# Attention, the normalisation behind it and the last MLP's first half put into one block of a fused two-layer kernel

## The chip, the core and the metric

The kernel runs on one core of a Trainium2 chip. A core has a matrix engine (TensorE, PE in the rows), a vector engine (VectorE, DVE), a scalar engine (ScalarE, ACT), a general engine (GpSimd, POOL) and a queue that here only starts transfers (SyncE, SP). They run side by side, each takes its own instructions strictly in order, and they wait for each other with semaphores. The metric is the time of one execution on the device, in microseconds (us).

## The reference, cut to what matters

Two layers, each of an attention-like part and an MLP, with a layernorm before and behind each part. The change touches the end of the second attention and the second MLP (x is 4 x 256 tokens of 512, in f32).

```python
x = x + _layernorm(_L1_attn_ref(_layernorm(x), Wq, Wkr, Wdk, Wupk, Wupv, Wo))   # 32 heads of 128, 8 groups
x = x + _layernorm(_L1_ffn_ref(_layernorm(x), w1, mean_w1, w2, mean_w2, w3, mean_w3))

def _binary_diff_weight(w, base):
    d = w - base
    return base + jnp.mean(jnp.abs(d)) * jnp.sign(d)
W1, W2, W3 = ...                                  # each from its pair, 512 x 1792 elements
h = jax.nn.silu(hidden @ W1.T) * (hidden @ W3.T)  # 1792 wide
return h @ W2.T
```

The three means are computed long before, and lie in a small tile (coeff).

## The kernel before, in words

The program is a row of phases. Each is a block with one instruction list for each engine, and a barrier of all engines closes it. Tokens lie as 8 tiles of 128 rows; four batches of 256 tokens are two tiles each. Every large matmul is done as three (high part by high part, low by high, high by low), from operands that ScalarE rounds (the high part) and GpSimd or VectorE subtracts (the low part).

**Attention** (`attention_phase`, L1222): 8 groups of heads times 4 batches are 32 units. `groups` writes group 0 and group 7 out and loops over the others. A unit b of TensorE's body is: the queries of the next unit (48 matmuls of 256 columns, L1297), the output product of the unit before (24 of 512 columns, L1322 to L1324), the transposes of the probabilities and their product with the values (`attend`, L1331 to L1344), and the scores of the next unit (L1308, L1310). Around it ScalarE copies half of the query product aside (`turn`, L1368), GpSimd multiplies it by the sines (L1423), VectorE multiplies by the cosines and adds both (`rotate`, L1456), takes the row maxima (L1461 to L1468), ScalarE does the exponentials (L1377, L1380), VectorE scales them (`probabilities`, L1474 to L1479) and adds the output product to `acc` (L1485). Once a group, GpSimd subtracts the low part of a weight (L1427, L1431). The last unit, (7, 3), has no queries of another unit to cover its softmax.

**"fc"** (`finish_phase` without a product): for each of the 8 token tiles, VectorE takes mean and variance of `acc` (L348 to L352), GpSimd the inverse root (L304), VectorE scales, adds to `x` (L373, L376), takes the moments of the new `x`, and normalises (L333); TensorE transposes (L223), ScalarE and VectorE split the result into `xh` and `xl` (L257, L338). The first two tiles of the MLP's weights are loaded at its start (L208).

**"md"** (`widen_phase`, kind "diff"): 14 tiles of 128 hidden channels. For each, GpSimd subtracts base from weight into `full` (L569), ScalarE takes the sign (L516), VectorE makes base + mean x sign in three parts (L598), ScalarE and GpSimd split two of them into `wh` and `wl` (L523, L564), the third is kept in `down`; TensorE does 48 matmuls of 512 columns (L503), ScalarE the silu (L552) and VectorE the product into `hidden` (L618). Weights, `full`, `wh` and `wl` are held twice, so that GpSimd subtracts two tiles ahead. **"fd"** then does the last product, its norm and the stores.

## Time and profile before

| | us |
|---|---|
| median of 3 runs | 1897.51 |
| lowest, highest | 1897.16, 1898.31 |
| the profiled execution's own time | 1897.62 |
| its span, first to last instruction | 1895.8 |
| TensorE busy in the span | 1677.3 (88%) |
| VectorE, ScalarE, GpSimd busy | 1153.1, 859.2, 814.2 |

The profile is of one execution. Its span is 1.8 us shorter than that execution's time. A timeline row gives the start, the duration, the engine, the source line, the operation, what it writes and reads, how many of them are merged in the row, and in brackets how long the engine was idle before it and who ended that. A row of windows gives, for a stretch, the busy time of each engine, the TensorE clock granted (1.00 is 2.4 GHz, 0.50 is 1.2 GHz) and the share of the DMA engines that was busy.

### The profile page before, as it was taken

What the parts mean: (1) busy time and instruction counts of PE and PEld (TensorE: products, weight loads), DVE (VectorE), ACT (ScalarE), POOL (GpSimd) and SP (SyncE); (2) the same over time, 40 slices, a digit from 0 to 9 for tenths busy, and PEclk for the clock granted to TensorE, in tenths of its full rate; (3) what the DMA queues carried; (4) which work ended last, traced back from release to release, by engine and by line L of the source; (5) the groups of instructions that cost most, each with busy time, mean ns of one, the idle gap of its engine ahead of it and who ended that gap; (6) DMA issues with size and microseconds to landing.
All of it is one profiled execution on the core that took longest, in us unless ns stands there. A gap on an engine that the chain in (4) does not pass through costs nothing. (4 is left out here: it accounts for less than half of the span.)

```text
span 1895.8 us, 24327 instructions
## 1 busy us (share of the span) xinstructions
PE 1677.3 (88%) x8118; PEld 1372.5 (72%) x8118; DVE 1153.1 (61%) x1614; ACT 859.2 (45%) x1743; POOL 814.2 (43%) x416
## 2 busy tenths in 40 slices
PE   5984889899997799898989999999999996399988
PEld 4852777787776688676877778778878784288867
DVE  4325999999996432452816666666675666546332
...
DMA packets 25185, 100.79 MB, mean 53 GB/s; under 512 B 3104, under 2 KB 3360, under 8 KB 22560
## 3 DMA queue, kind: packets, MB, share of 16 engines
...
## 5 line engine op out<-in xcount | busy, mean ns | idle before, releaser
L1423 POOL TENSOR_TENSOR stretch_turned<-stretch_turned,res_const 128x1024 f32<-128x1024 f32 x32 | 79.9, 2496 | 402.6 <-ACT stretch_turned L1369 402.6
L985 PE MATMUL psum<-scratch_s,res_const 128*128 128x256 f32 x1024 | 247.5, 380 | 4.0 <-DVE scratch_s L957 4.0
L985 PEld LDWEIGHTS psum<-scratch_s,res_const 128*128 128x128 f32 x1024 | 194.1, 190 | 32.2 <-DVE scratch_s L957 6.0
L858 POOL TENSOR_TENSOR scratch_s<-scratch_s,scan_cm 128x1024 f32<-128x1024 f32 x64 | 150.9, 2357 | 54.0 <-DVE scratch_s L947 54.0
L947 DVE TENSOR_TENSOR_SCAN scratch_s<-psum,scratch_s 128x512 f32<-128x512 f32 x128 | 155.3, 1213 | 4.4 <-ACT psum L899 4.2
L1297 PE MATMUL psum<-opnd_xh,query_wqh 128*128 128x256 f32 x512 | 151.3, 295 | 1.9 <-PEq L94 1.9
L846 POOL TENSOR_TENSOR scratch_s<-scan_bm,scratch_s 128x1024 f32<-128x1024 f32 x64 | 151.0, 2360 | 0.1
L899 ACT ACTIVATE psum<-ssm_dt,ssm_vec 128x255 f32 (+1 forms) x256 | 111.2, 466 | 80.3 <-DVE scratch_s L947 79.8
L1297 PE MATMUL psum<-opnd_xh,query_wql 128*128 128x256 f32 x512 | 145.6, 284 | 0.0
L1297 PE MATMUL psum<-opnd_xl,query_wqh 128*128 128x256 f32 x512 | 145.6, 284 | 0.0
L979 PE MATMUL psum<-scan_diag,scratch_s 128*128 128x256 f32 x512 | 133.2, 384 | 0.5 <-ACT scratch_s L891 0.5
L1377 ACT ACTIVATE stretch_pa<-psum,stretch_nm 128x128 f32<-128x128 f32 x128 | 45.3, 366 | 194.7 <-DVE stretch_nm L1468 194.7
L979 PEld LDWEIGHTS psum<-scan_diag,scratch_s 128*128 128x128 f32 x512 | 96.2, 193 | 13.0 <-ACT scratch_s L891 0.9
L1322 PE MATMUL psum<-stretch_woh,stretch_oh 128*128 128x512 f32 x256 | 100.3, 392 | 1.4 <-DVE stretch_ol L1501 1.4
L1297 PEld LDWEIGHTS psum<-opnd_xh,query_wqh 128*128 128x128 f32 x512 | 98.9, 193 | 3.2 <-issue 2.3
L1323 PE MATMUL psum<-stretch_wol,stretch_oh 128*128 128x512 f32 x256 | 100.0, 391 | 0.0
L1324 PE MATMUL psum<-stretch_woh,stretch_ol 128*128 128x512 f32 x256 | 99.9, 390 | 0.0
L1297 PEld LDWEIGHTS psum<-opnd_xl,query_wqh 128*128 128x128 f32 x512 | 98.8, 193 | 0.8
L1297 PEld LDWEIGHTS psum<-opnd_xh,query_wql 128*128 128x128 f32 x512 | 98.8, 193 | 0.0
L957 DVE TENSOR_TENSOR scratch_s<-psum,scan_cm 128x512 f32<-128x512 f32 x128 | 88.6, 692 | 14.2
L235 PE MATMUL psum<-stretch_wh,stretch_hh 128*128 128x512 f32 x176 | 71.0, 404 | 16.9 <-ACT stretch_wh L284 15.2
L503 PE MATMUL psum<-opnd_xh,mlp_wh 128*128 128x512 f32 x224 | 70.1, 394 | 14.9 <-POOL mlp_wl L564 14.9
...
## 6 DMA issues: line engine op xcount, KB each, us to landing
...
```

Of the source, the lines that this page charges most:

```text
L846: nc.gpsimd.tensor_tensor(by_state(shared[r][h]), bm[:, 4 * h:4 * h + 4, :], u[r].rearrange("p (a t) -> p a t", a=1).broadcast_to((P, 4, S ...
L858: nc.gpsimd.tensor_tensor(shared[r][h], shared[r][h], weights(4 * h, 4), ALU.mult).then_inc(weighted_pool, 1)
L899: ins = nc.scalar.activation(by_state(bank)[:, n, 1:SEQ], flat_dt[:, bass.ds(s * SEQ + 1, SEQ - 1)], ACT.Exp, scale=M.vec[:, bass.ds(s * N ...
L947: nc.vector.tensor_tensor_scan(quarter(r, i), decay_shared[i % 2], quarter(r, i), 0.0, ALU.mult, ALU.add).then_inc(scanned, 1)
L957: nc.vector.tensor_tensor(own[i], state[i], weights(NH + 2 * i, 2), ALU.mult).then_inc(weighted, 1)
L979: mm = nc.tensor.matmul(by_state(state[i])[:, :, t * P:(t + 1) * P], ut[r][:, t * P:(t + 1) * P], diag[:, t, 2 * i:2 * i + 2, :], start=Tr ...
L985: mm = nc.tensor.matmul(ps_y[r], ident, part[:, n * SEQ:(n + 1) * SEQ], start=False, stop=stop and (n + 1) * SEQ == part.shape[1])
L1297: mm = nc.tensor.matmul(ps_q[:, h * SEQ:(h + 1) * SEQ], w[:, k, h * HD:(h + 1) * HD], x[:, k, b * SEQ:(b + 1) * SEQ], start=(k == 0 and w ...
L1322: nc.tensor.matmul(X[t], oh[:, t, part], woh[:, h, :], start=(h == 0), stop=False)
L1323: nc.tensor.matmul(X[t], oh[:, t, part], wol[:, h, :], start=False, stop=False)
L1324: mm = nc.tensor.matmul(X[t], ol[:, t, part], woh[:, h, :], start=False, stop=(h == HPG - 1))
L1423: nc.gpsimd.tensor_tensor(heads(turned[:, :]), heads(turned[:, :]), over_heads(C_SIN, SEQ), ALU.mult).then_inc(q_sine, 1)
```

## The change

The phases of attention, "fc" and "md" become one block, `attention_mlp_phase`. The steps of "fc" and of the first MLP weights are written between the steps of attention's last group, and behind them. ScalarE applies both normalisations (`y_norm`, `x_norm`), GpSimd adds to `x` (`residual`). Weights are held in two slots, each with one raw and one base tile: the first slot lies over keys of groups 0 to 4, the second over the query weights. Difference, sign and sum are made in place in the raw tile. A slot is loaded again once its low part and its `down` part are made. MLP tiles 0 and 1 are run batch by batch (`widen_batch`, 24 matmuls of 256 columns for both products of a batch) as tokens become ready; tiles 2 to 13 as before, 48 matmuls each. GpSimd makes the difference of a tile behind the low part of the tile before. `ending(g, b, at)` is true in group 7 at unit b == at.

```diff
+    HALVES = ((0, 0, 2, 3), (1, 0, 4, 7), (0, 1, 5, 6), (1, 1, 2, 3))
+    ps_m = [[M.ps[:, 4 * s + 2 * a:4 * s + 2 * a + 2, :].rearrange("p a c -> p (a c)") for a in range(2)] for s in range(2)]
...
+            def load_mlp(f):
+                s = f % 2
+                if f == 0:
+                    sp.wait_ge(scored, U - BATCH)
+                if f == 1:
+                    sp.wait_ge(wo_lo, GROUPS)
+                    sp.wait_ge(q_prod, U)
+                at_least(sp, mw_lo, f - 1)
+                at_least(sp, mw_down, f - 1)
+                sp.dma_start(mw_raw[s][:, :], w_mlp[:, f * RC:(f + 1) * RC]).then_inc(mw_in[s], 16)
+                sp.dma_start(mw_base[s][:, :], b_mlp[:, f * RC:(f + 1) * RC]).then_inc(mw_in[s], 16)
+
...
+            for f in range(F1):
+                load_mlp(f)
...
+            def token_transposes(t):
+
+                pe.wait_ge(xn_ready, t + 1)
+                if t < 2:
+                    pe.wait_ge(q_turned, U)
+                    pe.wait_ge(q_cosine, U)
+                at_least(pe, x_lo, t - 1)
+                for c in range(KM):
+                    mm = nc.tensor.transpose(ps_t[t][:, c * P:(c + 1) * P], xn[t % 2][:, c * P:(c + 1) * P], ident)
+                mm.then_inc(transposed, 1)
...
+            def widen_into(out, f, a, lo, hi):
+                for k in range(KM):
+                    for w, x in ((mwh, M.xh), (mwh, M.xl), (mwl, M.xh)):
+                        mm = nc.tensor.matmul(out, w[f % 2][:, a, k, :], x[:, k, lo:hi],
+                                              start=(k == 0 and w is mwh and x is M.xh), stop=(k == KM - 1 and w is mwl))
+                return mm
...
+            def widen_batch(i, b):
+
+                f, _, *banks = HALVES[i]
+                pe.wait_ge(x_lo, QT * b + QT)
+                for a in range(2):
+                    mm = widen_into(M.ps[:, banks[a], (b % 2) * SEQ:(b % 2 + 1) * SEQ], f, a, b * SEQ, (b + 1) * SEQ)
+                if b % 2:
+                    mm.then_inc(half_prod, 1)
+
...
+            token_transposes(0)
+            token_transposes(1)
             output(GROUPS - 1, BATCH - 1)
+            weights_split(0)
+            pe.wait_ge(exped, U)
+            widen_batch(0, 0)
+            weights_split(1)
+            widen_batch(1, 0)
+            token_transposes(2)
+            token_transposes(3)
+            widen_batch(0, 1)
+            token_transposes(4)
+            token_transposes(5)
+            widen_batch(1, 1)
+            pe.wait_ge(added, 2 * U)
+            widen_batch(2, 2)
+            token_transposes(6)
+            pe.wait_ge(half_kept, 1)
+            widen_batch(3, 2)
+            token_transposes(7)
+            widen_batch(2, 3)
+            widen_batch(3, 3)
+            for f in range(2, F1):
+                weights_split(f)
+                at_least(pe, gated, f - 3)
+                at_least(pe, kept, f - 3)
+                for a in range(2):
+                    if f == 2 and a == 1:
+                        pe.wait_ge(half_kept, 4)
+                    widen(f, a)
 
...
+            def x_norm(t):
+                act.wait_ge(x_shifted, t // 2 + 1)
+                at_least(act, transposed, t - 1)
+                nc.scalar.activation(xn[t % 2][:, :], M.x[:, t, :], ACT.Identity, scale=of_tile(t, 20, 21),
+                                     bias=of_tile(t, 21, 22)).then_inc(xn_ready, 1)
...
+            def mlp_high(f):
+                act.wait_ge(mw_full, f + 1)
+                if f in (2, 3):
+                    act.wait_ge(half_prod, f + 1)
+                at_least(act, prod, 2 * (f - 3))
+                nc.scalar.activation(flat4(mwh[f % 2]), mw_raw[f % 2][:, 0:WC], ACT.Copy).then_inc(mw_hi, 1)
...
+                if ending(g, b, 1):
+                    difference_sign(0)
+                if ending(g, b, 2):
+                    y_norm(0)
+                    y_norm(1)
+                    mlp_high(0)
...
+                if ending(g, b, BATCH - 1):
+                    x_norm(0)
+                    x_norm(1)
...
+                if ending(g, b, 2):
+                    difference_sign(1)
...
+            token_high(0)
+            token_high(1)
+            y_norm(2)
+            y_norm(3)
+            mlp_high(1)
+            y_norm(4)
+            y_norm(5)
+            x_norm(2)
+            x_norm(3)
+            token_high(2)
+            token_high(3)
+            y_norm(6)
+            y_norm(7)
+            x_norm(4)
+            x_norm(5)
+            token_high(4)
+            token_high(5)
+            gate_half(0)
+            x_norm(6)
+            x_norm(7)
+            token_high(6)
+            gate_half(1)
+            token_high(7)
+            difference_sign(2)
+            gate_half(2)
+            mlp_high(2)
+            gate_half(3)
+            difference_sign(3)
+            mlp_high(3)
+            for f in range(2, F1):
+                if f >= 3 and f + 1 < F1:
+                    difference_sign(f + 1)
+                    mlp_high(f + 1)
+                gate(f)
...
+            def residual(t):
+                pool.wait_ge(y_normed, t + 1)
+                nc.gpsimd.tensor_tensor(M.x[:, t, :], M.x[:, t, :], acc[:, t, :], ALU.add).then_inc(x_new, 1)
...
+            def difference(f):
+                pool.wait_ge(mw_in[f % 2], 32 * (f // 2 + 1))
+                nc.gpsimd.tensor_tensor(mw_raw[f % 2][:, :], mw_raw[f % 2][:, :], mw_base[f % 2][:, :], ALU.subtract).then_inc(mw_diff, 1)
+
+            def mlp_low(f):
+                pool.wait_ge(mw_hi, f + 1)
+                nc.gpsimd.tensor_tensor(flat4(mwl[f % 2]), mw_raw[f % 2][:, 0:WC], f32(flat4(mwh[f % 2])), ALU.subtract).then_inc(mw_lo, 1)
...
+                if ending(g, b, 0):
+                    difference(0)
+                if ending(g, b, 2):
+                    difference(1)
+                    residual(0)
+                    residual(1)
+                    mlp_low(0)
...
+            x_scale(0)
+            y_scale(1)
+            y_scale(2)
+            residual(2)
+            residual(3)
+            x_scale(1)
+            residual(4)
+            residual(5)
+            mlp_low(1)
+            x_scale(2)
+            y_scale(3)
+            residual(6)
+            residual(7)
+            x_scale(3)
+            for f in range(2, F1):
+                difference(f)
+                mlp_low(f)
...
+            def whole(f):
+                dve.wait_ge(mw_sign, f + 1)
+                for a, lo, hi in ((0, 0, WC // 2), (1, WC // 2, WC)):
+                    part = mw_raw[f % 2][:, lo:hi]
+                    ins = nc.vector.scalar_tensor_tensor(part, part, M.coeff[:, a:a + 1], mw_base[f % 2][:, lo:hi], ALU.mult, ALU.add)
+                ins.then_inc(mw_full, 1)
...
+            def keep_half(i):
+                f, h, _, bank = HALVES[i]
+                dve.wait_ge(half_prod, i + 1)
+                dve.wait_ge(half_gated, i + 1)
+                nc.vector.scalar_tensor_tensor(hidden[:, f, h * HALF:(h + 1) * HALF], M.ps[:, bank, :], 1.0,
+                                               mid[:, h * HALF:(h + 1) * HALF], ALU.mult, ALU.mult).then_inc(half_kept, 1)
...
+                if last:
+                    y_moments_of(1)
...
+                if ending(g, b, 1):
+                    y_moments_of(0)
+                    whole(0)
+                    y_shift(0)
+                if ending(g, b, 2):
+                    values(g, b + 1, v + 1)
+                    accumulate(v, b)
+                    x_moments_of(0)
+                if more(g, b):
                     probabilities(*after(g, b))
+                if ending(g, b, 2):
+                    x_shift(0)
...
+            y_shift(1)
+            y_moments_of(2)
+            token_low(0)
+            token_low(1)
+            whole(1)
+            y_shift(2)
+            x_moments_of(1)
             accumulate(U - 1, BATCH - 1)
+            y_moments_of(3)
+            x_shift(1)
+            x_moments_of(2)
+            token_low(2)
+            token_low(3)
+            y_shift(3)
+            x_shift(2)
+            whole_down(0)
+            whole_down(1)
+            x_moments_of(3)
+            token_low(4)
+            token_low(5)
+            keep_half(0)
+            x_shift(3)
+            token_low(6)
+            keep_half(1)
+            token_low(7)
+            whole(2)
+            whole_down(2)
+            keep_half(2)
+            whole(3)
+            whole_down(3)
+            keep_half(3)
+            for f in range(2, F1):
+                if f >= 3 and f + 1 < F1:
+                    whole(f + 1)
+                    whole_down(f + 1)
+                keep(f)
+            dve.wait_ge(kept, F1 - 2)
...
-    attention_phase(nc, M, place, wq_raw, wqh, wql, K, V, acc, D["w_q"], D["w_o"])
-    M.acc = acc
+    down1, hidden1, mid1 = at("down1", 48)("down", [P, F1, DM]), at("hidden1", 100)("hidden", [P, F1, TOK]), at("mid1", 76)("mid", [P, TOK])
+    early, later = at("mlpa", 80), at("mlpb", 176)
+    mw_raw, mw_base = [p("raw", [P, RC]) for p in (early, later)], [p("base", [P, RC]) for p in (early, later)]
+    mwh, mwl = [p("wh", [P, 2, KM, P], F32R) for p in (early, later)], [p("wl", [P, 2, KM, P], F32R) for p in (early, later)]
+    norm = at("norm", 196)
+    xn = [norm(f"xn{i}", [P, DM]) for i in range(2)]
+    attention_mlp_phase(nc, M, place, wq_raw, wqh, wql, K, V, acc, D["w_q"], D["w_o"], D["w_mlp"], D["b_mlp"], hidden1, down1, mid1,
+                        mw_raw, mw_base, mwh, mwl, xn)
     if stop_after == "att": return M
...
-    widen_phase(nc, "md", M, mlp1, F1, "diff", D["w_mlp"], D["b_mlp"], hidden=hidden1, coeff=M.coeff, second=(down1,),
-                raw=mlp_raw, base=mlp_base)
-    M.hidden, M.down = hidden1, down1
-    if stop_after == "md": return M
-    last = Stretches(nc, (z + 16 * KB, z + 48 * KB), (z + 132 * KB, end))
+    last = Stretches(nc, (z + 16 * KB, z + 48 * KB), (z + 76 * KB, z + 100 * KB), (z + 156 * KB, end))
```

On GpSimd, at the end of the attention, there stood before (L1423 sines, L1431 low part of the output weight, L304 inverse roots, then L569 the first differences):

```order
L1431 TENSOR_TENSOR stretch_wol<-query_raw,stretch_woh 128x2048
L1423 TENSOR_TENSOR stretch_turned<-stretch_turned,res_const 128x1024 x2
L1272 UNCONDITIONAL_BRANCH
L93 ISA
L288 UNCONDITIONAL_BRANCH
L304 TENSOR_TENSOR fc_small<-fc_small,res_half 128x1 x16
L202 UNCONDITIONAL_BRANCH
L93 ISA
L557 UNCONDITIONAL_BRANCH
L569 TENSOR_TENSOR mlp_full_11215<-mlp_raw_85,mlp_base_87 128x1536
L569 TENSOR_TENSOR mlp_full_11216<-mlp_raw_86,mlp_base_88 128x1536
L564 TENSOR_TENSOR mlp_wl_11212<-mlp_full_11215,mlp_wh_11210 128x1024
```

and there stand now, from the sines of unit (7, 2) on (L1627 and L1635 inverse roots, L1639 difference, L1631 residual, L1643 low part of an MLP weight):

```order
L1615 TENSOR_TENSOR stretch_turned<-stretch_turned,res_const 128x1024
L1627 TENSOR_TENSOR stretch_ln<-stretch_ln,res_half 128x2
L1615 TENSOR_TENSOR stretch_turned<-stretch_turned,res_const 128x1024
L1639 TENSOR_TENSOR mlpb_raw<-mlpb_raw,mlpb_base 128x1536
L1631 TENSOR_TENSOR tok_x<-tok_x,acc_acc 128x512 x2
L1643 TENSOR_TENSOR mlpa_wl<-mlpa_raw,mlpa_wh 128x1024
L1635 TENSOR_TENSOR stretch_ln<-stretch_ln,res_half 128x2
L1627 TENSOR_TENSOR stretch_ln<-stretch_ln,res_half 128x2 x2
L1631 TENSOR_TENSOR tok_x<-tok_x,acc_acc 128x512 x2
L1635 TENSOR_TENSOR stretch_ln<-stretch_ln,res_half 128x2
L1631 TENSOR_TENSOR tok_x<-tok_x,acc_acc 128x512 x2
L1643 TENSOR_TENSOR mlpb_wl<-mlpb_raw,mlpb_wh 128x1024
```

What moved: the difference of the second weight tile stands right behind the sines of the last unit, and the low part of tile 1 behind four residuals.

On VectorE, in the last units, there stood before (L1468 negated maxima, L1474 to L1479 probabilities, L1490 values, L1485 `acc`):

```order
L1468 TENSOR_SCALAR stretch_nm<-stretch_mx 128x8
L1474 RECIPROCAL stretch_inv<-stretch_sums 128x8
L1477 TENSOR_SCALAR stretch_pa<-stretch_pa,stretch_inv 128x128 x4
L1479 TENSOR_SCALAR stretch_pb<-stretch_pb,stretch_inv 128x256 x4
L1490 COPY stretch_vs<-att_v 128x256
L1485 TENSOR_TENSOR acc_acc<-psum,acc_acc 128x512 x2
L1496 COPY stretch_pt<-psum 128x512
L1501 TENSOR_TENSOR stretch_ol<-psum,stretch_oh 128x512 x2
L1485 TENSOR_TENSOR acc_acc<-psum,acc_acc 128x512 x2
```

and there stand now:

```order
L1706 TENSOR_SCALAR stretch_nm<-stretch_mx 128x8
L1788 COPY stretch_vs<-att_v 128x256
L1723 TENSOR_TENSOR acc_acc<-psum,acc_acc 128x512 x2
L1742 BN_STATS stretch_ln<-tok_x 128x6 x2
L1745 BN_AGGR stretch_ln<-stretch_ln 128x2 x2
L1747 TENSOR_SCALAR stretch_ln<-stretch_ln 128x2
L1712 RECIPROCAL stretch_inv<-stretch_sums 128x8
L1715 TENSOR_SCALAR stretch_pa<-stretch_pa,stretch_inv 128x128 x4
L1717 TENSOR_SCALAR stretch_pb<-stretch_pb,stretch_inv 128x256 x4
L1751 SCALAR_TENSOR_TENSOR stretch_ln<-stretch_ln 128x2
L1800 COPY stretch_pt<-psum 128x512
L1728 BN_STATS stretch_ln<-acc_acc 128x6 x2
```

What moved: the copy of the values, the adds into `acc` and the moments of the new `x` stand ahead of the last unit's probabilities; moments of `acc` stand behind the copy of a transposed block.

## Rows read from the trace of the kernel before

**Rows 1.** The page's first part: busy time, share, instructions of each engine.

```profile
PE 1677.3 (88%) x8118; PEld 1372.5 (72%) x8118; DVE 1153.1 (61%) x1614; ACT 859.2 (45%) x1743; POOL 814.2 (43%) x416
```

**Rows 2.** Busy time by stretch: "fc" and the lead-in, "md", the end.

```profile
1595.50:1647.40 51.90, 8.91 (x32) 5.71 (x32) 39.35 (x85) 8.69 (x11) 20.16 (x19) 0.54 0.21 79
1647.40:1801.90 154.50, 154.44 (x672) 126.91 (x672) 70.51 (x52) 44.92 (x40) 74.12 (x25) 0.99 0.31 117
1801.90:1895.80 93.90, 78.69 (x337) 64.40 (x336) 28.61 (x55) 26.28 (x30) 40.07 (x16) 0.93 0.06 23
```

**Rows 3.** Timeline of TensorE: the last scores, the last softmax, the two gaps behind.

```profile
1570.51 1.05 PE L1308 MATMUL psum<-att_k,stretch_q 128*128 128x128 f32 x8
1571.40 1.89 PE L1310 MATMUL psum<-att_k,stretch_q 128*128 128x256 f32 x8
...
1582.31 0.72 PE L1331 MATMUL psum<-res_const,stretch_pa 128*128 128x128 f32 x4 [3.53 <-DVE stretch_pb L1479]
...
1603.02 1.11 PE L223 MATMUL psum<-res_const,fc_xn 128*128 128x128 f32 x4 [7.57 <-DVE fc_xn L333]
```

**Rows 4.** Timeline of all engines, from the first difference to the first MLP matmul.

```profile
1635.06 6.80 POOL L569 TENSOR_TENSOR mlp_full<-mlp_raw,mlp_base 128x1536 f32<-128x1536 f32 x2 [4.27 <-POOLq L94]
1638.51 1.48 ACT L516 ACTIVATE mlp_full<-mlp_full 128x1536 f32<-128x1536 f32 x1 [5.34 <-POOL mlp_full L569]
1640.03 3.04 DVE L598 SCALAR_TENSOR_TENSOR mlp_full<-mlp_full,res_coeff,mlp_base 128x512 f32<-128x512 f32 x2 [6.13 <-ACT mlp_full L516]
...
1643.76 1.06 ACT L523 ACTIVATE mlp_wh<-mlp_full 128x1024 fp32r<-128x1024 f32 x1 [3.77 <-DVE mlp_down L598]
...
1644.97 2.35 POOL L564 TENSOR_TENSOR mlp_wl<-mlp_full,mlp_wh 128x1024 fp32r<-128x1024 f32 x1 [3.11 <-ACT mlp_wh L523]
...
1647.46 0.77 PE L503 MATMUL psum<-opnd_xh,mlp_wh 128*128 128x512 f32 x1 [14.92 <-POOL mlp_wl L564]
```

**Rows 5.** Timeline of TensorE: the first and the last query matmul of a unit.

```profile
1443.97 0.47 PE L1297 MATMUL psum<-opnd_xh,query_wqh 128*128 128x256 f32 x1
...
1449.80 0.28 PE L1297 MATMUL psum<-opnd_xh,query_wql 128*128 128x256 f32 x1
```

**Rows 6.** Timeline of all engines, where GpSimd's subtraction met VectorE's rotation.

```profile
1416.15 4.53 POOL L1427 TENSOR_TENSOR query_wql<-query_raw,query_wqh 128x2048 fp32r<-128x2048 f32 x1
...
1417.36 4.40 DVE L1456 TENSOR_TENSOR stretch_q<-stretch_direct,stretch_turned 128x1024 f32<-128x1024 f32 x1
...
1421.91 0.85 PE L1308 MATMUL psum<-att_k,stretch_q 128*128 x4 [2.05 <-DVE stretch_q L1456]
```

**Rows 7.** Busy time by stretch: around that stall, and after the last softmax.

```profile
1418.00:1422.00 4.00, 1.95 (x6) 0.65 (x4) 4.00 (x2) 1.19 (x2) 2.68 (x1) 1.00 0.16 33
1422.00:1425.50 3.50, 3.50 (x13) 3.09 (x14) 0.96 (x2) 0.00 (x0) 0.00 (x0) 0.55 0.65 262
```

**Rows 8.** Timeline of VectorE: the probabilities and the rotation of unit (7, 3).

```profile
1562.16 0.20 DVE L1474 RECIPROCAL stretch_inv<-stretch_sums 128x8 f32<-128x8 f32 x1 [3.40 <-ACT stretch_pb L1380]
1562.40 0.87 DVE L1477 TENSOR_SCALAR stretch_pa<-stretch_pa,stretch_inv 128x128 f32<-128x128 f32 x4
1563.19 1.14 DVE L1479 TENSOR_SCALAR stretch_pb<-stretch_pb,stretch_inv 128x256 f32<-128x256 f32 x4
...
1568.11 1.22 DVE L1456 TENSOR_TENSOR stretch_q<-stretch_direct,stretch_turned 128x1024 f32<-128x1024 f32 x1
```

**Rows 9.** Timeline of all engines: moments and inverse root of a tile in "fc".

```profile
1597.08 0.69 DVE L348 BATCH_NORM_STATS2 fc_small<-acc_acc 128x6 f32<-128x512 f32 x1 [0.90 <-PEq L94]
1597.81 0.18 DVE L350 BATCH_NORM_AGGREGATE fc_small<-fc_small 128x2 f32<-128x6 f32 x1
1598.03 0.15 DVE L352 TENSOR_SCALAR fc_small<-fc_small 128x1 f32<-128x1 f32 x1
...
1598.26 0.55 POOL L304 TENSOR_TENSOR fc_small<-fc_small,res_half 128x1 f32<-128x1 f32 x1 [31.46 <-DVE fc_small L352]
```

**Rows 10.** Groups of instructions by line, in "md": count, busy, mean ns.

```profile
L598 DVE SCALAR_TENSOR_TENSOR mlp_full<-mlp_full,res_coeff,mlp_base 128x512 f32<-128x512 f32 x28 | 51.2, 1868 | 8.6 <-ACT mlp_full L516 8.6
L569 POOL TENSOR_TENSOR mlp_full<-mlp_raw,mlp_base 128x1536 f32<-128x1536 f32 x14 | 49.7, 3552 | 33.5 <-DMA mlp_base<-in_b_mlp 29.2 <-POOLq L94 4.3
L564 POOL TENSOR_TENSOR mlp_wl<-mlp_full,mlp_wh 128x1024 fp32r<-128x1024 f32 x14 | 33.6, 2401 | 39.5 <-ACT mlp_wh L523 39.5
L257 ACT ACTIVATE opnd_xh<-psum 128x512 fp32r<-128x512 f32 x8 | 4.8, 597 | 39.5 <-PE psum L223 39.5
```

**Rows 11.** Timeline of VectorE in "md": two parts of a weight, with GpSimd idle.

```profile
1661.48 1.41 DVE L598 SCALAR_TENSOR_TENSOR mlp_full<-mlp_full,res_coeff,mlp_base 128x512 f32<-128x512 f32 x2
```

**Rows 12.** The base tile's transfers: time from issue to landing.

```profile
DMA to landing us min/median/max: 5.4/5.6/8.5
```

118 lines of the change are left out of this document (108 added, 10 removed).

## The prediction, made before the changed kernel was run

> **What bounds the kernel now.** I read the page's shares first: TensorE is busy 88% of the span, VectorE 61%, the others under half [rows 1]. Then the stretches from the end of attention on [rows 2], since the change touches nothing ahead of attention's last group. In "md" TensorE is busy 154.4 of 154.5 us: it is the bound there, and nothing that leaves its 672 matmuls alone can shorten that stretch. In the 51.9 us ahead of it TensorE is busy 8.9 us, with the 32 transposes of "fc", at about half clock (0.54). So the time to be had is this hole, from the end of the last output product (1595.45) to the first MLP matmul (1647.46), 52.0 us. The timeline tells what fills it: 7.57 us until the first transpose, then seven more tiles that VectorE paces, busy for 39.4 us of it [rows 2, 3], then the block's end and a serial chain that makes the first weight: two differences 6.80, sign 1.48, three parts, high part 1.06, low part 2.35, with 14.92 us idle on TensorE [rows 4]. The part behind "md" (93.9 us) keeps its work and its lead-in, since the last tile's product must be whole there too.
>
> **What the change removes, and what TensorE's own work becomes.** The whole hole of 52.0 goes. Its eight transposes stay: at full clock 0.46 each (half of the 0.9 that a row of 1.11 takes up at 1.2 GHz [rows 3]). Two of them fall in the 1.4 us in which TensorE waits for the last low part anyhow; six cost 2.8. The matmuls of tiles 0 and 1 become 8 batches of 24 with 256 columns. The queries are the same form: 47 of them from 1443.97 to 1449.80, so 0.124 each with the first, 0.12 after it [rows 5], 2.92 a batch. Eight batches 23.4, twelve tiles of 48 x 0.2275 (660 in 150.0 us) 131.0: together 154.4, as before.
>
> **The last units of attention get longer.** (a) In unit (7, 2) VectorE has, between maxima and probabilities, 3.40 us of waiting [rows 8]. Moments of two tiles (2 x 0.72 + 2 x 0.2 + 0.1 = 1.94, from starts in [rows 9]), two parts of a weight 1.41 [rows 11] and the shift, which waits for GpSimd's root (0.55), come to 4.2: the probabilities are 0.8 to 1.0 late. TensorE starts on them 2.2 us after their end today, so this is hidden. (b) GpSimd now goes from the sines (about 1565.3 to 1567.8) straight to the difference of slot 1. Its load is released by the last queries (1561.1) and lands some 6.0 later (0.4 between issues, 5.6 [rows 12]), at 1567.2. So the difference starts at 1567.8 and ends at 1571.3, and VectorE's rotation, now at 1568.11 [rows 8], comes behind it. The trace has this collision: behind the 4.53 us subtraction the rotation took 4.40 in place of 1.22, and TensorE idled 2.05 [rows 6]. Here rotation ends at 1572.5, scores begin at 1572.6, not 1570.51: 2.1 late. After the idle 2.05 the granted clock was 0.55 for 3.5 us [rows 7]; my stall is 1.5, near enough that I take half clock for the scores, +1.6 (0 if it holds). (c) Ahead of the last probabilities stand the adds into `acc`, which need the second half of output (7, 2), and the moments of x, 1.94. Scores end 1576.7, that output 1582.2, adds 1583.0, moments 1585.0, x's root on GpSimd 0.5, reciprocal and scaling 2.2 [rows 8]: TensorE starts at about 1587.8, today at 1582.31 [rows 3]. The 0.5 us that the transposes wait for adds today goes; two normalisations of 0.6 on ScalarE (nearest row: 0.597 [rows 10]) ahead of the high parts take it back. So the last product ends 5.5 late, at 1600.9. Bounds: 1.5 (load lands after the rotation, clock held) to 8.
>
> A rule of the Trainium skill speaks against the change here. The row above shows the rotation, with two SBUF inputs, standing still until GpSimd's instruction ended [rows 6]. The page "SBUF — State Buffer", section "Who interferes with whom", says that such VectorE instructions and a GpSimd instruction that reads SBUF share a port by an exclusive lock: the later one blocks for the whole instruction. The change puts 13 reading instructions of GpSimd (8 residuals, 3 differences, 2 low parts) among VectorE's two-input steps. With the lock I get the sum below; without it no collision would cost anything and the time would be about 1863.
>
> **Behind the last product, gap by gap** (start of each wait from the sum so far).
> 1. Batch 0 of tile 0 runs at once, 1600.9 to 1603.8. For batch 0 of tile 1 the low part of weight 1 must be made. VectorE is free of attention at 1595.4 and does: shift 0.2, moments 1.96, two low parts 1.2, a wait for a residual on GpSimd 0.8, two parts of weight 1 1.4, shift 0.2, moments of x 2.6 (one more wait for a residual); then GpSimd: root 0.6, residuals 4 and 5 (not in the trace; 512 columns, half of the 2.40 low part [rows 10] with a little more, 1.24 each) 2.5, lock 0.3, low part 2.4. Sum 14.2, to 1609.7: **5.9 idle**.
> 2. Batch at half clock, +1.65. Transposes 2 and 3; their high and low parts (0.6 + 0.6 + 0.6): **1.8 idle**, +1.65 for the clock.
> 3. Batches (1, 1) and (2, 2) have their tokens. Transpose 6 waits for the last shift, which waits behind the difference of tile 2 (3.5, lock): **0.5 idle**. Transpose 7, its high and low part ahead of batch 3: **1.6 idle**.
> 4. Weight 2 may be rounded only when batch (2, 3) has read slot 0: silu 0.6, high 1.06, low 2.4, hand-overs 0.4, less the 2.9 of the last batch: **1.6 idle**.
> 5. The second half of tile 2 waits for the last half kept, and VectorE's order puts weight 3 ahead of it: difference 3.5, sign 1.48, three parts 2.1, keep 0.65, after low part 2: 7.9, against 5.5 of matmul: **2.5 idle**, +1.65 for the clock.
> Gaps 13.9, clock 4.95.
>
> **The steady part.** Difference f + 1 now follows low part f on GpSimd, so the weights are one serial loop: 3.5 + 1.48 + 1.41 + 1.06 + 2.40 and hand-overs of 0.02, 0.04, 0.04, 0.15 and 0.1 [rows 4, 10, 11] = 10.2 a tile, under the 10.9 of TensorE. A weight is ready about 4 us ahead. The load (6.0) lies beside it, in the other slot. Here the two collisions of today's "md" (parts of 1.87 in the mean, 0.71 alone [rows 10, 11]) should be gone, for GpSimd is idle while VectorE makes the parts. Cost 0, bounds 0 to 1.6 a tile.
>
> **The sum.** Against 52.0 removed stand 5.5 + 2.8 + 13.9 + 4.95 = 27.1. Net 24.9 faster: the last MLP matmul ends at 1776.9, not 1801.8. From the profiled execution's 1897.6 (span 1895.8 and 1.8 around it, 0.1 from the median) this gives **1872.7**.
>
> **The rivals.**
> - *Gaps cheaper* (chance 0.16): the clock holds in gaps under 2 us, or the load lands behind the rotation. The clock terms (4.95 + 1.6) or about 4 of the first stage go, down to 1863. For: only stalls of 2.05 and more are seen with a fall. Against: several gaps here follow close on each other.
> - *Half clock through the whole middle* (0.12): "fc" shows 0.54 with sparse work [rows 2]. If TensorE, 60% busy from 1600 to 1642, stays at 1.2 GHz, the eight batches cost up to 2.92 more each; 15 of these 23 are not in my sum or hidden: 1888.
> - *The loop of weights becomes the bound* (0.04), the one that ends slower. If VectorE's parts still meet GpSimd and take 1.87 each as today, the loop is 10.2 + 2.3 = 12.5: 1.6 idle in each of 12 tiles, 19; with a half-clock stretch of 1.65 after every second one, 10; and 2.3 more in gap 5: about 1904. It is slower than before once the loop passes some 12.3. Against: in the new order GpSimd has nothing to do while the parts are made.
> - *The change doesn't do what it says* (0.02): the weights of slot 0 are late, as the load is held by a wait, and most of the hole comes back: 1893 to 1898. Against: its only wait, all scores of group 6, is over 60 us ahead of need.
> - Forecast as summed, 1867 to 1880: 0.60; between it and these, 0.06.
>
> **How the numbers follow.** The forecast is the likeliest case, 1872.7. The range 1863 to 1888 takes in the cheaper gaps and the half clock, and leaves out the slow loop and part of the mixed cases. A measurement of this kernel tells 0.2%, 3.8 us, from no change. Faster by more: 0.60 + 0.16 + 0.12 + 0.06 + 0.01 = 0.95; same 0.01; slower 0.04.
>
> **What the profile of the changed kernel would show.** The windows should show TensorE idle some 14 us between the last output product and tile 3, and none from there to the last MLP matmul. The rotation of unit (7, 3) should take about 4 us beside a difference of 3.5 on GpSimd, and its scores wait 1.5. The last softmax should leave TensorE idle about 5.5, not 3.53. The wait ahead of tile 1, batch 0, should be the longest, on GpSimd's low part. Parts of weights from tile 4 on should take 0.71 each. I am wrong if TensorE waits on low parts in tiles 4 to 13, if the granted clock is 0.5 through the batches, or if VectorE's moments slow down beside GpSimd, which no row here excludes.

## The result, and the profile of the changed kernel

The changed kernel takes 1865.9 us, the median of 4 runs (1864.2 to 1867.5). The kernel before, beside it, takes 1897.3 (1896.5 to 1898.3). The ratio is 0.983, with a 95% interval of 0.982 to 0.985: 31.4 us less, where the forecast was 24.9 less. 1865.9 lies inside the range of 1863 to 1888, but near its fast end and outside the 1867 to 1880 to which the prediction gave 0.60. The profiled execution took 1867.5 us.

First the shares. TensorE is busy as long as before [rows 1], but the span around it is 30.1 us shorter:

```profile
PE 1676.6 (90%) x8214; PEld 1377.9 (74%) x8214; DVE 1114.2 (60%) x1592; ACT 872.7 (47%) x1761; POOL 818.6 (44%) x416
```

The two traces of the changed kernel differ by 2.7 us ahead of the changed part (the stall below ends at 1499.38 in one and at 1496.69 in the other). So the traces are laid over each other at the last stall that they all share, ahead of scores that start at 1498.15 before and at 1499.38 after: the first row here is of the kernel before, the second of the changed one (timeline of TensorE; start, duration, what runs, idle ahead of it and who ended it). The third and fourth rows are the first matmul behind the MLP's first half, before and after; start minus idle is the end of the last MLP matmul, 1801.92 and 1771.44.

```profile
1498.15 1.04 PE L1308 MATMUL psum<-att_k,stretch_q 128*128 x7 [2.04 <-DVE stretch_q L1456]
```

```profile
1499.38 0.82 PE L1350 MATMUL psum<-att_k,stretch_q 128*128 x5 [2.04 <-DVE stretch_q L1694]
```

```profile
1810.63 0.77 PE L235 MATMUL psum<-stretch_wh,stretch_hh 128*128 128x512 f32 x1 [8.71 <-ACT stretch_wh L284]
```

```profile
1780.45 0.77 PE L235 MATMUL psum<-stretch_wh,stretch_hh 128*128 128x512 f32 x1 [9.01 <-ACT stretch_wh L284]
```

The changed trace is 1.2 us late at the shared stall. Set that off, and the last MLP matmul ends at 1770.2, which is 31.7 us earlier than before and 6.7 earlier than the 1776.9 of the sum. Below, a time "from the shared stall" is the stretch from the start of that stall to the last MLP matmul: 305.8 us before, 274.1 after.

TensorE's timeline shows what replaced the hole of 52 us [rows 2 to 4]:

```profile
1573.62 1.16 PE L1350 MATMUL psum<-att_k,stretch_q 128*128 128x128 f32 x8 [1.69 <-DVE stretch_q L1694]
...
1586.46 1.11 PE L1373 MATMUL psum<-res_const,stretch_pa 128*128 128x128 f32 x4 [4.47 <-DVE stretch_pb L1717]
...
1607.30 0.36 PE L1402 MATMUL psum<-opnd_xh,mlpb_wh 128*128 128x256 f32 x1 [4.57 <-issue]
...
1614.35 0.39 PE L1402 MATMUL psum<-opnd_xh,mlpa_wh 128*128 128x256 f32 x1 [1.57 <-DVE opnd_xl L1755]
...
1625.74 0.66 PE L1396 MATMUL psum<-res_const,norm_xn 128*128 128x128 f32 x4 [1.64 <-ACT norm_xn L1509]
...
1631.12 0.38 PE L1402 MATMUL psum<-opnd_xh,mlpa_wh 128*128 128x256 f32 x1 [1.41 <-DVE opnd_xl L1755]
...
1638.43 0.47 PE L1402 MATMUL psum<-opnd_xh,mlpa_wh 128*128 128x512 f32 x1 [1.30 <-POOL mlpa_wl L1643]
...
1646.03 0.50 PE L1402 MATMUL psum<-opnd_xh,mlpa_wh 128*128 128x512 f32 x1 [1.91 <-DVE hidden_hidden L1778]
```

The first is the wait for the rotation, the second the last softmax (3.53 before [rows 3]). The six behind the last output product, behind which the first batch starts at 1599.70, sum to 12.4 us. The row of the longest, 4.57, names no releaser ("issue"); GpSimd's low part of weight 1 ended 0.1 us before it, at 1607.20. From 1646.03 on TensorE doesn't wait, as the second of these stretches says (columns as in [rows 2]):

```profile
1599.70:1646.00 46.30, 33.91 (x241) 31.60 (x239) 24.36 (x46) 20.24 (x26) 19.79 (x13) 0.96 0.27 103
1646.00:1771.40 125.40, 125.38 (x552) 103.56 (x552) 33.41 (x41) 37.85 (x32) 60.79 (x21) 1.00 0.32 113
1771.40:1865.70 94.30, 78.80 (x337) 64.68 (x336) 28.66 (x55) 26.29 (x30) 40.09 (x16) 0.94 0.06 23
```

The parts of the weights, where [rows 10] had a mean of 1868 ns, are now made while GpSimd stands idle (groups by line, 1646 to 1771):

```profile
L1762 DVE SCALAR_TENSOR_TENSOR mlpa_raw<-mlpa_raw,res_coeff,mlpa_base 128x512 f32<-128x512 f32 x10 | 7.0, 746 | 0.3 <-ACT mlpa_raw L1518 0.3
```

### The profile page after: what moved, and what is told of

Its sections match the earlier page's. It is cut to its first block and busy times, and to the rows that moved or that the text cites. A ratio compares the mean times of both kernels' runs of the same rounds, so it can differ in the third digit from the quotient of the medians.

```text
span 1865.7 us, 24304 instructions
## 1 busy us (share of the span) xinstructions
PE 1676.6 (90%) x8214; PEld 1377.9 (74%) x8214; DVE 1114.2 (60%) x1592; ACT 872.7 (47%) x1761; POOL 818.6 (44%) x416
## 5 line engine op out<-in xcount | busy, mean ns | idle before, releaser
L951 DVE TENSOR_TENSOR_SCAN psum<-scan_decay,psum 128x512 f32<-128x512 f32 x64 | 77.0, 1204 | 0.0
```

## The experiments

My theory after the result had four claims. (1) The gain is in two layers of about equal size, the steps and the loads that lie over attention; the batches give little. (2) Each wait that is left belongs to one order on one engine, and goes alone. (3) The 1.7 us ahead of the scores is the collision of rotation and subtraction. (4) Half clock follows an idle of 2.05 us or more. The rivals: a wait taken away comes back at the next one; the new order behind attention is the gain; the clock goes by something else. Ten kernels ran. Their times are the medians of 4 or 5 runs (10 for one); the ratio is to the kernel before, run beside them. They ran in three sets, and the kernel before took 1898.4, 1897.4 and 1896.6 in them. So a difference between medians of different sets can be off by up to 1.8 us, and where a difference is small, the last column counts. It is of one trace each, and its share of half clock varies by itself by a few tenths.

| kernel | us | the kernel before, beside it | ratio, 95% interval | from the shared stall |
|---|---|---|---|---|
| before | 1897.3 | | 1 | 305.8 |
| steps and loads behind attention | 1893.95 | 1897.4 | 0.998 (0.997 to 0.999) | 302.2 |
| steps behind attention | 1880.2 | 1897.4 | 0.991 (0.990 to 0.993) | 287.4 |
| longer idle, 5.30 | 1872.7 | 1898.4 | 0.986 (0.984 to 0.987) | 280.6 |
| no batches in between | 1868.5 | 1897.4 | 0.985 (0.984 to 0.987) | 277.1 |
| longer idle, 2.55 | 1868.2 | 1897.4 | 0.984 (0.983 to 0.986) | 275.1 |
| changed kernel, again | 1865.9 | 1898.4 | 0.983 (0.981 to 0.984) | 271.5 |
| rotation first | 1863.7 | 1898.4 | 0.981 (0.980 to 0.983) | 271.4 |
| last half kept first | 1863.2 | 1896.6 | 0.982 (0.981 to 0.984) | 272.3 |
| weight 1 early | 1860.0 | 1898.4 | 0.980 (0.979 to 0.981) | 267.9 |
| five reorderings | 1851.0 | 1896.6 | 0.976 (0.975 to 0.977) | 260.8 |

The changed kernel's first trace, which has the collision of claim (3), has 274.1 in the last column.

**The changed kernel again.**

> The changed kernel once more, beside the variants, so that they are compared on one chip. Both theories: 1865 to 1868 us; TensorE idle about 4.5 us ahead of batch (1, 0), 1.3 to 1.9 us at each of the later gaps, and 1.00 of the clock from 1612 us on.

Measured: 1865.9 (1862.1 to 1867.9). This profiled execution, 1862.1 us, had no idle ahead of the scores at all. VectorE's rotation started 0.05 us ahead of GpSimd's subtraction, and this time GpSimd stood still, its subtraction taking 4.46 us (timeline of this run):

```profile
1566.64 1.22 DVE L1694 TENSOR_TENSOR stretch_q<-stretch_direct,stretch_turned 128x1024 f32<-128x1024 f32 x1
```

```profile
1566.69 4.46 POOL L1639 TENSOR_TENSOR mlpb_raw<-mlpb_raw,mlpb_base 128x1536 f32<-128x1536 f32 x1 [1.35 <-DMA mlpb_base<-in_b_mlp]
```

In the trace of the first run, GpSimd was ahead by 0.31 us, and VectorE stood still:

```profile
1569.06 3.43 POOL L1639 TENSOR_TENSOR mlpb_raw<-mlpb_raw,mlpb_base 128x1536 f32<-128x1536 f32 x1 [0.97 <-DMA mlpb_base<-in_b_mlp]
...
1569.37 4.20 DVE L1694 TENSOR_TENSOR stretch_q<-stretch_direct,stretch_turned 128x1024 f32<-128x1024 f32 x1
```

Both subtractions start behind the load of the base tile, as their rows say, so which of the two it is hangs on when that load lands, to a few tenths of a microsecond. The other traces in which it was open (weight 1 early, both longer idles, no batches, last half first) have the 1.5 to 1.9 us. The rest of the expectation held: 4.59, 1.57, 1.60, 1.41, 1.30, 1.88 idle.

**Rotation first.** An undo of the collision alone, on GpSimd:

```diff
                 if ending(g, b, 2):
+                    pool.wait_ge(q_done, U)
                     difference(1)
```

> GpSimd's subtraction for weight 1 waits until VectorE's rotation for unit (7, 3) is done; nothing else is changed. Theory (the rotation stands still behind the subtraction): the rotation takes 1.22 us instead of 4.20, the 1.69 us idle of TensorE ahead of the scores goes, and since no other resource holds attention there, the end moves by 1.5 to 1.7 us: about 1864.4. Rival 1 (the 1.7 us are slack, given back at the last probabilities, which wait for moments of x and residuals): the idle moves to the last softmax, the time stays within 0.4 us of the changed kernel. Rival 2 (rotation is slow for another reason, such as its load): it still takes about 4 us.

Measured: 1863.7 (1860.9 to 1865.2), 2.2 less in the median; the ranges of the two kernels overlap, so the trace has to carry it. The rotation takes 1.22 and the subtraction 3.45 behind it (timelines of VectorE and GpSimd, this run), and no idle is left ahead of the scores:

```profile
1569.57 1.22 DVE L1695 TENSOR_TENSOR stretch_q<-stretch_direct,stretch_turned 128x1024 f32<-128x1024 f32 x1
```

```profile
1570.87 3.45 POOL L1639 TENSOR_TENSOR mlpb_raw<-mlpb_raw,mlpb_base 128x1536 f32<-128x1536 f32 x1 [2.58 <-DVE stretch_q L1695]
```

The next wait, the last softmax, is 4.55 in place of 4.47: it gave back 0.08 and not 1.7. The stretch from the shared stall is 271.4, as in the execution that happened to miss the collision, and 2.7 under the one that had it. 2.0 of this lie ahead of the softmax wait, 1.7 of them the idle. The other 0.7 is a shorter run of half clock behind the last softmax, whose transposes and products took 6.4 us (1584.80 to 1591.16) where they took 7.1 (1586.46 to 1593.55). That part isn't shown to be the collision's: from the end of the softmax wait to the end of the last output product it is 12.6 to 12.8 us in the three traces without the collision, and between 12.9 and 13.6 in the six with it. The theory holds, both rivals fall, and the collision costs 2.0 us and up to 0.7 more.

**Weight 1 early.** Weight 1's parts go behind the last probabilities on VectorE, its high part between two copies on ScalarE, its low part ahead of the residuals on GpSimd:

```diff
 ScalarE, body of (7, 3)
                 nc.scalar.activation(pt[:, 0, :], X[2], ACT.Copy).then_inc(p_kept_act, 1)
+                if ending(g, b, BATCH - 1):
+                    mlp_high(1)
...
 GpSimd
             x_scale(0)
+            mlp_low(1)
             y_scale(1)
...
             residual(5)
-            mlp_low(1)
...
 VectorE
                 if ending(g, b, 2):
                     x_shift(0)
+                    whole(1)
...
             token_low(1)
-            whole(1)
```

> The three steps that make weight 1 (its parts on VectorE, its high part on ScalarE, its low part on GpSimd) are moved ahead of the last softmax's tail, to fill waits inside unit (7, 3); everything else keeps its order. Theory (the idle 4.57 us ahead of batch (1, 0) is the queueing of these three steps behind the norms of tokens 2 to 5, and the half-clock stretch after it is paid on top): that idle falls under 0.5 us, the batch behind it runs at full clock in about 2.9 us instead of 4.6, and of these 6.2 us some 4 to 6 are kept, since transposes of later tokens then wait a little more: 1860 to 1862. Rival (TensorE waits for tokens 2 and 3 next, so the wait is only moved): the sum of idle between 1600 and 1650 us stays at 12 us, and only the clock term of 1.7 us or nothing is gained: 1864 to 1866.

Measured: 1860.0 (1858.5 to 1861.4), 5.9 less. In the changed kernel this chain led to the idle of 4.57 (timeline of all engines but TensorE):

```profile
1596.44 2.99 POOL L1631 TENSOR_TENSOR tok_x<-tok_x,acc_acc 128x512 f32<-128x512 f32 x2
1596.82 3.16 DVE L1762 SCALAR_TENSOR_TENSOR mlpb_raw<-mlpb_raw,res_coeff,mlpb_base 128x512 f32<-128x512 f32 x2
...
1600.02 1.06 ACT L1525 ACTIVATE mlpb_wh<-mlpb_raw 128x1024 fp32r<-128x1024 f32 x1 [4.33 <-DVE mlpb_raw L1762]
...
1602.41 2.49 POOL L1631 TENSOR_TENSOR tok_x<-tok_x,acc_acc 128x512 f32<-128x512 f32 x2
...
1604.85 2.35 POOL L1643 TENSOR_TENSOR mlpb_wl<-mlpb_raw,mlpb_wh 128x1024 fp32r<-128x1024 f32 x1
```

Moved up, the low part is done at 1589.7, some 11 us ahead of its use, and TensorE goes through both batches, the output product and the transposes without a wait and at full clock (busy time by stretch, weight 1 early):

```profile
1592.10:1604.50 12.40, 12.36 (x80) 11.16 (x80) 10.34 (x27) 5.08 (x8) 7.66 (x8) 1.00 0.01 2
```

The stretch from the shared stall is 6.2 us shorter than in the changed kernel's first trace (both have the collision), which is 4.57 and the 1.7 of the half-clock batch. The later idles are 1.57, 1.67, 1.41, 1.30, 1.90, as before: nothing came back. The rival, that tokens 2 and 3 would be next, falls.

**A longer idle.** Two needless instructions ahead of the down part of weight 3, which delay the last keep and with it the second half of tile 2:

```diff
             whole(3)
+            for spare in range(2):
+                nc.vector.scalar_tensor_tensor(down[:, 9 + spare, :], mw_raw[1][:, WC:RC], ...)
             whole_down(3)
             keep_half(3)
```

> Two needless instructions of VectorE (each the size of the down part of a weight, their result never read) stand ahead of the down part of weight 3, so that the last idle of the stretch, 1.91 us, becomes about 3.3 us. It adds work and leaves nothing out. Theory (the granted clock falls after an idle of 2.05 us or more, as ahead of the change, and stays at 1.00 after 1.91): the clock is seen near 0.5 for 3 to 4 us behind this idle, so the time is longer by 1.4 plus 1.6 to 1.9, in all 3.0 to 3.3 us: about 1869. Rival (the clock had held because of the dense batches ahead, and not because of the idle's length): it stays at 1.00, and the time is longer by 1.4 us alone: about 1867.4.

Measured: 1872.7, and the idle is 5.30, not 3.3 (TensorE's row first, then VectorE's: the down part met GpSimd's low part of 2.35 us, and took 2.83 instead of 0.75).

```profile
1649.16 0.79 PE L1402 MATMUL psum<-opnd_xh,mlpa_wh 128*128 128x512 f32 x1 [5.30 <-DVE hidden_hidden L1778]
```

```profile
1645.68 2.83 DVE L1771 SCALAR_TENSOR_TENSOR down_down<-mlpb_raw,res_coeff,mlpb_base 128x512 f32<-128x512 f32 x1
```

```profile
1649.20:1653.00 3.80, 3.80 (x9) 3.02 (x10) 0.00 (x0) 2.17 (x2) 2.62 (x1) 0.50 0.86 306
1653.00:1660.00 7.00, 7.00 (x27) 5.65 (x27) 2.25 (x3) 0.33 (x1) 0.00 (x0) 0.84 0.15 61
```

The clock was 0.50 behind it, and 0.84 in the mean of the next 7 us; that is half clock for about 6.0 us (3.8, and 0.32 of 7.0), a cost of 3.0. With the 3.4 of idle it explains the 6.5 us from the shared stall. But at 5.30 the run doesn't tell theory and rival apart: the idle was too long. So it was made again, with one such instruction.

> As the run with the longer idle, with one needless instruction of VectorE in place of two. That run showed 5.30 us of idle where 3.3 was meant, since the second instruction pushed the down part of weight 3 behind the start of GpSimd's low part (2.83 us instead of 0.75). With one instruction the down part begins ahead of it, and the idle should be 1.91 + 0.67 = 2.6 us. Theory (an idle of 2.05 us and more was followed by half clock ahead of the change, so 2.6 will be): granted clock near 0.5 for some 3.5 us behind it, 0.67 + 1.6 to 1.9 longer than the changed kernel: 1868 to 1869. Rival (only idles above 4 us lower it in this place, after dense batches): clock 1.00, 0.7 longer: 1866.5 to 1867.

Measured: idle 2.55 us, and the clock held (busy time by stretch, behind that idle):

```profile
1647.40:1650.90 3.50, 3.50 (x15) 2.91 (x16) 0.00 (x0) 1.03 (x1) 3.50 (x2) 1.00 0.25 44
```

The median, 1868.2, is just what the theory said, and the theory is wrong all the same: the row says 1.00. The stretch from the shared stall is 275.1, only 1.0 above the changed kernel's first trace, 0.64 of it the added idle and the rest small differences of both signs. What else makes the median's distance isn't shown; the other three executions have no trace. The rival named the clock of this trace rightly, but its reason (only idles above 4 us) fell as well. With the steps behind attention the same last idle was 1.89 us and the clock held; with the loads behind it too, it was again 1.89 us, behind the same matmuls, and the clock fell (busy time by stretch, one row of each of these two runs, in this order):

```profile
1657.30:1660.80 3.50, 3.47 (x15) 2.90 (x16) 0.00 (x0) 1.03 (x1) 3.50 (x2) 1.00 0.16 18
```

```profile
1671.80:1675.30 3.50, 3.50 (x9) 2.79 (x10) 0.00 (x0) 1.02 (x1) 3.50 (x2) 0.54 0.20 25
```

**Steps behind attention.** `y_norm`, `x_norm`, moments, shifts, residuals, differences, signs and splits that stand inside units (7, 1) to (7, 3) go behind `groups(...)`, on four engines. Their order stays, but for VectorE, where `y_shift(0)` now comes ahead of `whole(0)`, and the last copy of values and the adds into `acc` are back in their old places. On TensorE:

```diff
+            output(GROUPS - 1, BATCH - 1)
             token_transposes(0)
             token_transposes(1)
-            output(GROUPS - 1, BATCH - 1)
```

> The steps of norms and of weights 0 and 1 that stand inside units (7, 1) to (7, 3) are put behind attention on all four engines, in the same order; the loads of both weights still run during attention, and the two tiles still run batch by batch. Theory (about half of the gain is that these steps lie over the last units of attention): the last output product ends some 3 us earlier, but TensorE then idles 8 to 10 us ahead of the first transpose, and 8 us ahead of the first batch of tile 1; the end is 12 to 15 us later than the changed kernel, 1878 to 1881. Rival (the overlap is paid back, since it delays attention by the collisions and by the moments ahead of the last probabilities): at most 5 us later, 1866 to 1871.

Measured: 1880.2 (1878.9 to 1882.7), 14.3 above the changed kernel. The last softmax wait is 3.53 again, as before, and the two big idles are where they were expected, the second shorter than its 8 (timeline of TensorE, this run):

```profile
1603.19 1.97 PE L1396 MATMUL psum<-res_const,norm_xn 128*128 128x128 f32 x8 [7.97 <-ACT norm_xn L1509]
...
1617.30 0.55 PE L1402 MATMUL psum<-opnd_xh,mlpb_wh 128*128 128x256 f32 x1 [6.29 <-issue]
```

So the steps over attention are worth 13.3 us of the stretch, after what they cost inside it, the collision included; against the trace that missed the collision it is 15.9.

**Steps and loads behind attention.** The same, and on SyncE:

```diff
                 if f == 0:
-                    sp.wait_ge(scored, U - BATCH)
+                    sp.wait_ge(scored, U)
+                    sp.wait_ge(o_prod, 2 * U)
```

> As the one before, and the loads of weights 0 and 1 wait for attention's last output product too, so that nothing of the MLP's lies over attention. Theory (the wait for a load of 8.5 us and a subtraction of 3.5 behind it then stand ahead of everything on GpSimd): 11 to 13 us later than with the loads alone ahead, 1889 to 1893; of the gain of 31 us only some 7 are left, which is the pipelining of norms, weights and two tiles behind attention. Rival 1 (the weights are needed only at batch 0 of tile 1, and the norms that VectorE paces hide them): 0 to 4 us later than the run before. Rival 2 (the new order behind attention is the main gain, 20 us or more): 1878 or less.

Measured: 1893.95 (1891.7 to 1895.2), 13.8 above the one before; of the gain 3.5 us are left (0.2%), where 7 were expected. The idle ahead of the first transposes is 21.70, 13.7 more; GpSimd waited for the base of weight 0 (timelines of GpSimd and of TensorE):

```profile
1602.29 3.42 POOL L1636 TENSOR_TENSOR mlpa_raw<-mlpa_raw,mlpa_base 128x1536 f32<-128x1536 f32 x1 [34.97 <-DMA mlpa_base<-in_b_mlp]
```

```profile
1617.67 0.69 PE L1397 MATMUL psum<-res_const,norm_xn 128*128 128x128 f32 x2 [21.70 <-ACT norm_xn L1510]
```

The clock's fall shown above is in the trace's time too, some 1.6 us. Without it, by my estimate, the new order behind attention would be worth about 5 us (3.5 + 1.6), and the early loads about 13 (302.2 - 287.4 - 1.6). What in the new order gives the 5 us, the batches apart, no run takes apart.

**No batches in between.** All transposes, then eight batches; gates and keeps of the first halves behind the last token:

```diff
-            widen_batch(0, 0)
+            for t in range(2, TT):
+                token_transposes(t)
...
-            token_transposes(2)
-            token_transposes(3)
+            widen_batch(0, 0)
```

> All eight transposes are run first, then the eight batches of tiles 0 and 1 with nothing between them; the gates and keeps of the first halves follow the last token on ScalarE and VectorE. The rest keeps its order. Theory (what sets the time in this stretch is the chain of norms and of the weights, on the other engines, and TensorE has slack; without batches in between it idles longer ahead of transposes, but the norms are not held up by gates and keeps): the idle only changes its place, within 3 us of the changed kernel either way, 1864 to 1869. Rival (the batches fill TensorE's waits with 12 us of matmuls, which would come on top if they stood behind the last token): 8 to 12 us later, 1874 to 1878.

Measured: 1868.5 (1868.3 to 1870.3), 2.7 more; from the shared stall 3.0, against the changed kernel's first trace. The idle is nearly the same, 13.4 in place of 12.4, but it comes in larger pieces, 6.27, 3.74 and 2.78, with only transposes between them, and TensorE is at half clock through them and into the first batches (busy time by stretch, this run):

```profile
1597.50:1616.00 18.50, 5.77 (x25) 5.00 (x26) 13.22 (x35) 11.42 (x16) 12.29 (x10) 0.63 0.39 150
1616.00:1646.60 30.60, 30.03 (x217) 28.73 (x216) 8.14 (x12) 9.14 (x10) 7.49 (x4) 0.95 0.18 65
```

The 0.63 of the first is carried by the part without work; each group of eight transposes took 1.94 to 1.97 us, where it takes 1.04 at full clock. So the batches are worth 3 us, and most of that is the clock. The rival's 8 to 12 us aren't there. That the norms pace this stretch fits the idles, each of which ends with ScalarE's `xn`, the normalised tile.

**Last half kept first.**

```diff
             keep_half(2)
+            keep_half(3)
             whole(3)
             whole_down(3)
-            keep_half(3)
```

> One reordering on VectorE: the last kept half of tile 2 (0.69 us) stands ahead of the parts of weight 3. Theory (the last idle of 1.91 us is this order alone, and no clock term comes with it, as short idles were not followed by half clock here): the idle goes, 1.7 to 1.9 us less, 1863.9 to 1864.3. Rival (my sum's: half clock follows it, so 1.65 more would be had): 1862.4.

Measured: 1863.2 (1862.6 to 1864.0), 2.6 less in the median, but only 0.8 more under the kernel before beside it (33.3, where the changed kernel again was 32.6 under), and 1.85 less from the shared stall than the changed kernel's first trace (0.17 of it a shorter wait in the collision, which both traces have). TensorE has no idle there any more, the idle was 1.91, and nothing was had beyond it. The median lies between the two forecasts and doesn't tell them apart; the trace does, with the stretch shorter by the idle alone.

**Five reorderings at once.** The three above, and two more: `mlp_high(2)` ahead of `gate_half(2)` on ScalarE, and on GpSimd

```diff
             x_scale(3)
+            pool.wait_ge(x_shifted, 4)
             for f in range(2, F1):
                 difference(f)
```

> Five reorderings at once, no step left out: the subtraction for weight 1 waits for the rotation; the parts, high and low part of weight 1 are made ahead of the last softmax's tail; the last kept half of tile 2 stands ahead of weight 3's parts on VectorE; the high part of weight 2 ahead of a gate on ScalarE; GpSimd's difference for weight 2 waits for the last token's shift. Theory (each idle of the stretch belongs to one order on one engine and clears by itself): 1.7 (of which half is there in the mean, since the collision at the rotation does not come in each execution, so 1 to 1.7) + 5.9 as measured with weight 1 early + 1.9 + 0.5 + 1.7 less what comes back: 9 to 12 us under the changed kernel, 1854 to 1857. Rival (the waits behind the first are linked, the sum of idle stays once weight 1 is early): 1858 to 1860, as with weight 1 alone.

Measured: 1851.0 (1849.9 to 1852.3), ratio 0.976 (0.975 to 0.977): 46 us under the kernel before, and 15 under the changed one, or 13 if each is taken against the kernel before beside it. That is under the 1854 to 1857 expected. From the shared stall it is 10.7 under the changed kernel's second trace, which missed the collision, and 13.3 under its first, which had it. The sum's terms, before anything comes back, are 10.0 without the collision (5.9 + 1.9 + 0.5 + 1.7) and 11.7 with it, so nothing came back, and the traces gained 0.7 and 1.6 more than that. TensorE's stretches from the last output product on:

```profile
1593.90:1624.10 30.20, 26.37 (x217) 25.66 (x216) 16.73 (x40) 15.24 (x21) 14.08 (x11) 1.00 0.27 106
1624.10:1754.90 130.80, 130.76 (x576) 108.03 (x576) 36.25 (x45) 40.17 (x34) 64.30 (x22) 1.00 0.33 121
```

3.8 us of idle are left between 1593.9 and 1624.1 (30.20 less 26.37), against 12.4, and the clock is 1.00 throughout. The idles of 1.69, 4.57, 1.64 and 1.91 are gone and the 1.30 is 0.88; the 1.57 and the 1.41, which none of the five orders aims at, are left as they were. The last two reorderings ran only here, so what each gives alone isn't shown. The last softmax wait, 4.54, is the largest left.

## Why the prediction was right, and where its numbers were off

**The mechanism was right.** The hole of 52.0 went, and its place was taken by a later last product, gaps and transposes, in the order in which the sum had them. The longest gap is the one ahead of tile 1, batch 0, and ends 0.1 us behind GpSimd's low part; with the low part made earlier, it went. In the frame of before (the changed trace less 1.2 us), with the first batch's start at 1599.70 taken as the last output product's end, and TensorE's work behind it as 33.91 + 125.38, of which 154.4 were there before and 1.7 are the half clock:

| term | forecast | measured |
|---|---|---|
| last output product late | 5.5 | 3.0 |
| six transposes and the batches' own work | 2.8 | 3.2 |
| gaps behind it | 13.9 | 12.4 |
| half clock behind gaps | 4.95 | 1.7 |
| sum (the hole of 52.0 less the gain) | 27.1 | 20.3 |

**The step that failed is the clock.** The sum laid half clock on four places: the scores behind the stall of the rotation (1.6), and the work behind the gaps 1, 2 and 5 (1.65 each). Only the one behind gap 1 was there, at 4.57 idle; the batch took 4.6 us and not 2.9. The others had idles of 1.69, 1.57 and 1.91, and full clock behind each (busy time by stretch, the changed kernel):

```profile
1573.60:1576.10 2.50, 2.48 (x15) 2.32 (x16) 1.17 (x2) 0.00 (x0) 2.50 (x3) 1.00 0.02 7
...
1607.30:1611.90 4.60, 4.60 (x26) 4.60 (x27) 0.00 (x0) 0.00 (x0) 1.34 (x2) 0.63 0.01 4
1614.35:1617.85 3.50, 3.50 (x29) 3.50 (x30) 2.10 (x5) 2.94 (x4) 2.56 (x2) 1.00 0.46 119
...
1646.00:1649.50 3.50, 3.48 (x15) 2.91 (x16) 0.00 (x0) 1.03 (x1) 3.50 (x2) 1.00 0.13 16
```

That is 1.6 + 3.3 = 4.9 us, most of the 6.7. The error lies in the reading of before. The sum took the clock from one stall of 2.05 us with a fall behind it [rows 6, 7]. The same stall stands at the end of six attention groups, and the sum rests on one of the six. Behind the other five the clock was 1.00; here are two of them and the one that was used (busy time by stretch, the kernel before):

```profile
1347.35:1350.85 3.50, 3.50 (x23) 3.29 (x24) 1.63 (x3) 0.00 (x0) 0.00 (x0) 1.00 0.69 272
1421.90:1425.40 3.50, 3.49 (x13) 3.14 (x14) 1.06 (x2) 0.00 (x0) 0.00 (x0) 0.56 0.69 269
1498.15:1501.65 3.50, 3.50 (x23) 3.29 (x24) 1.63 (x3) 0.00 (x0) 0.00 (x0) 1.00 0.66 267
```

One in six was the price to be read there: 0.3 us for such a stall, not 1.65. The rival "gaps cheaper" said that the clock would hold, with a chance of 0.16 and a time down to 1863, on the argument that only stalls of 2.05 and more are seen with a fall. It was the nearer one in the clock's part, but its argument takes 2.05 for a price too. The sum without its four clock terms (6.55) is 1866.1, and 1865.9 was measured; that this is so near is luck, since one of the four came and the gaps and the end of attention were shorter by about as much.

**The end of attention** was 3.0 late. The rotation did take 4.20 beside the subtraction, and the scores waited 1.69 (forecast: some 4, and 1.5). The moments of `x` stood ahead of the last probabilities; the softmax wait was 4.47, not 5.5. Besides the 1.6 of the clock the sum had 0.9 too much there. "Rotation first" puts the collision at 1.7 us of idle, at 2.0 up to the softmax wait, and at 2.7 at most. That it was there at all hangs on the load: of seven traces in which it was open, one missed it.

The rotation standing still agrees with the rule that the prediction took from the Trainium skill ("SBUF — State Buffer", "Who interferes with whom"): whichever of the two came first ran at its own speed, by 0.31 us in one trace and by 0.05 in the other. By the same section, an instruction with one SBUF input doesn't contend outside VectorE's 2-port modes, and `tensor_scalar` is among those that can enter such a mode. The moments have one input and didn't wait: 1.28 us for two at 1602.78, beside GpSimd's residuals of 2.49. The small `tensor_scalar` behind them did (last section).

**The gaps** were 4.57, 1.57, 1.64, 1.41, 1.30, 1.91 where the sum had 5.9, 1.8, 0.5 + 1.6, 1.6, 2.5. The chain of weight 1 had the links that the sum lists, a microsecond shorter, and the lock fell on another pair: the parts (3.16 instead of 1.4) beside the residuals, instead of on the low part. Transpose 6, with 0.5 in the sum, waited 1.64, the only gap above its forecast; the others were 2.6 shorter together. The sum had the cause right, the last shift behind the difference of weight 2. That shift, 0.15 us alone, took 3.18 (timeline of VectorE, the changed kernel), and with the difference behind it in "Five reorderings" it took 0.15 and the gap went:

```profile
1621.67 3.18 DVE L1751 SCALAR_TENSOR_TENSOR stretch_ln<-stretch_ln 128x2 f32<-128x2 f32 x1
```

**The steady part** cost nothing, as forecast: parts of 746 ns, low parts ready 4.2 to 4.6 us ahead, no idle in 125.4 us. The rival "loop becomes the bound" fell with these two numbers, and "half clock through the whole middle" with 1.00 in every stretch from 1614 on.

**The tail** was taken as unchanged; it is 94.3 in place of 93.9, with 9.01 idle in place of 8.71. In all: 6.7 earlier than the sum, less 1.2 of this execution's late start and 0.4 of the tail, is 5.1; between the forecast's span, 1870.9, and 1865.7 lie 5.2.
